# Cross attention and a mixture of LoRA experts: transfers in quarter tiles of 64 partitions with one of each kind in flight, and a fold of squares in wider matmuls

## The reference

```python
def xattn(q, k, v):                  # q = layernorm(x), k = v = ctx, 8 heads of 64 channels
    qh = softmax(q over the 64 channels of a head)
    kh = softmax(k over the 2048 positions)
    kvs = einsum('bnhd,bnhe->bhde', kh, vh)
    return einsum('bnhd,bhde->bnhe', qh, kvs)
x = x + xattn(layernorm(x), ctx, ctx)
flat = layernorm(x).reshape(-1, 2048)
logits = flat @ router_w.T           # 4 experts, the 2 largest kept, softmax over them: gates
mid = einsum('tf,erf->ter', flat, A) # rank 16 for each expert
x = x + einsum('te,teo->to', gates, einsum('ter,eor->teo', mid, B)) * 4
```

## Time and profile before

| what | value |
|---|---|
| median of 3 runs | 493.88 us (493.44 to 500.45) |
| the profiled execution, its own time | 496.45 us |
| its span | 494.7 us |
| mean granted TensorE clock | 0.92 of full speed |
| busy share PE, DVE, POOL, ACT | 84%, 77%, 73%, 61% |
| moved by DMA | 137.99 MB, mean 279 GB/s |

### The profile page before, as it was taken

The page is one execution under the profiler, slowest core; times in us unless marked ns, Lnnn a source line. Parts: engine busy times, 40 slices in busy tenths (PEclk is TensorE's granted clock), DMA queues, the critical chain, the costliest instruction groups (busy, mean ns, idle before and its releaser), DMA issues.

```text
span 494.7 us, 22911 instructions
## 1 busy us (share of the span) xinstructions
PE 416.6 (84%) x9960; PEld 362.5 (73%) x9960; DVE 378.6 (77%) x1045; ACT 300.2 (61%) x404; POOL 358.8 (73%) x341
## 2 busy tenths in 40 slices
PE   6659888988978887887988896898897878999975
PEld 6648777877867676776877675787776767788864
DVE  2488758896868967887897876868895978976864
ACT  1367767766648566574867665666674848586410
POOL 0459978987869767877797876867895987898510
PEclk9657978999989988999899997988998999999997
DMA  8997877899899888999899997899997998755347
GB/s 300 416 366 219 295 225 258 257 298 326 260 315 291 237 315 277 288 315 299 298 280 350 294 303 248 251 310 301 336 302 227 326 296 284 247 177 207 121 187 256
DMA packets 38996, 137.99 MB, mean 279 GB/s; under 512 B 4208, under 2 KB 6384, under 8 KB 38768
## 3 DMA queue, kind: packets, MB, share of 16 engines
q1 hardware_dynamic: 38896, 136.52, 82.3%
HBM read 102.95 MB, written 33.55 MB: 276 GB/s over the span
## 4 chain that ended last, share of the span: by engine, by line
PE 72%; issue 12%; DVE 7%; DMA 4%; SPq 3%; POOL 1%; ACT 1%; DVEq 0%; POOLq 0%
PE num_ps L404 17%; PE kv_ps L384 15%; PE raw_ps L421 13%; PE delta_ps L469 10%; PE kv_ps L436 7%; PE delta_ps L470 6%; DMA ctx_sb<-in_ctxt_dram 4%; DVE y_sb L705 2%; DVE attnT L696 2%; PE kv_ps L369 2%; SPq L234 1%; PE raw_ps L455 1%; PE num_ps L361 1%; DVE bn_parts L638 1%; SPq L229 1%
## 5 line engine op out<-in xcount | busy, mean ns | idle before, releaser
L322 POOL TENSOR_TENSOR y_sb<-attnT,y_sb 128x512 f32<-128x512 f32 x128 | 164.2, 1283 | 68.1 <-DVE attnT L696 67.4
L310 POOL TENSOR_TENSOR ek_sb<-ctx_sb,kmax_row 128x512 f32<-128x512 f32 x128 | 167.4, 1309 | 41.5 <-ACT kmax_row L502 40.8
L705 DVE TENSOR_TENSOR y_sb<-delta_ps,y_sb 128x512 f32<-128x512 f32 x128 | 87.4, 685 | 55.9 <-PE delta_ps L470 54.9
L404 PE MATMUL num_ps<-kv_sb,x_sb 64*64 64x65 f32 x4096 | 97.3, 233 | 18.4 <-issue 11.8
L384 PE MATMUL kv_ps<-ctx_sb,ek_sb 128*64 128x65 f32 x2048 | 100.3, 241 | 14.3 <-issue 14.0
L404 PEld LDWEIGHTS num_ps<-kv_sb,x_sb 64*64 64x64 f32 x4096 | 78.1, 142 | 34.2 <-issue 20.3
L384 PEld LDWEIGHTS kv_ps<-ctx_sb,ek_sb 128*64 128x64 f32 x2048 | 79.6, 146 | 28.4 <-issue 17.8
L421 PE MATMUL raw_ps<-w_sb,y_sb 128*64 128x69 f32 x2048 | 93.5, 232 | 6.8 <-issue 6.8
L621 DVE TENSOR_REDUCE max_n<-ctx_sb 128x32 f32<-128x512 f32 x128 | 86.4, 677 | 11.1 <-DMA ctx_sb<-in_ctxt_dram 11.1
L696 DVE TENSOR_TENSOR attnT<-num_ps,rden 128x512 f32<-128x512 f32 x128 | 88.5, 691 | 4.5
L469 PE MATMUL delta_ps<-midT,b_hi 128*128 128x256 f32 x256 | 84.2, 349 | 3.8 <-issue 3.1
(11 more groups left out here) (62 smaller groups left out, 423.6 us busy)
## 6 DMA issues: line engine op xcount, KB each, us to landing
ctx_sb<-in_ctxt_dram SPq DMA_DIRECT2D x64, 520.0 KB, 5.5
x_sb<-in_x_dram SPq DMA_DIRECT2D x64, 512.0 KB, 6.3
y_sb<-in_xt_dram SPq DMA_DIRECT2D x64, 512.0 KB, 6.5
out_dram<-y_sb SPq DMA_DIRECT2D x60, 512.0 KB, 6.0
out_dram<-y_sb SPq DMA_DIRECT2D x8, 256.0 KB, 3.6
sq_a<-in_bt_dram SPq DMA_DIRECT2D x1, 1024.0 KB, 15.8
w_sb<-in_wt_dram SPq DMA_DIRECT2D x1, 552.0 KB, 9.5
cst<-in_consts_dram SPq DMA_DIRECT2D x1, 145.0 KB, 2.4
```

Of the source, the lines that this page charges most:

```text
L310: pool.tensor_tensor(ek_sb[:, t % 2, chunks(g), :].rearrange("p (a b) c -> p a b c", b=2), ctx_sb[:, t % 4, 2 * g:2 * g + 2, 1:P + 1, :].r ...
L322: pool.tensor_tensor(y, attnT[:, g, :], y, ALU.add).then_inc(x1_made, 1)
L404: mm = pe.matmul(num_ps[n, h, j * (DH + 1):(j + 1) * (DH + 1)], x_sb[d, t % 4, c * P + half * DH:c * P + (half + 1) * DH], kv_sb[d, t % 2, ...
L705: dve.tensor_tensor(y, delta_ps[i % 2][:].rearrange("p (j t c) -> p t j c", j=2, t=2), y, ALU.add).then_inc(out_made, 1)
```

## The change

Two things change.

First, the transfers. A tile of each stream moves in four pieces: two halves of the row (`k`) by two halves of the partitions (`part`, 64 each). The pieces are 256 KB (260 KB for ctx). SP's loop has a step of one quarter, with one piece of each stream in it. Each piece waits until the previous piece of its own stream has landed (`out_piece`, `x_piece`, `xt_piece`, `ctx_piece`). The waits for PE change as well: store and y no longer wait for `raw_done`; x waits for `num_done` up to the quarter that PE runs at the same q; ctx is issued two quarters later in the loop (offset 14 for 16) and waits for `kv_done` of the quarter of the same q. The loads ahead of the loop are cut in the same four pieces, but without waits.

Second, the squares. `fold_squares` makes four matmuls of 384 columns (three chunks for each group of 32 partitions) and four of 128 columns that add the fourth chunk, into columns 128 to 511 of the bank. `sq_sum` has three parts of 128 columns, ACT copies 384 columns, and `sum_squares` has three matmuls for one.

The consumers' counts of landed pieces go from 32 to 64 for each use of a buffer; this is left out below.

```diff
         attnT = sb("attnT", [P, 4, W])
         sq_a = sb("sq_a", [P, 2, H2])
         sq_b = sb("sq_b", [P, H2])
-        sq_sum = sb("sq_sum", [P, 2, P])
+        sq_sum = sb("sq_sum", [P, 2, 3, P])
         junk = sb("junk", [P, N], BF16)
         max_n = sb("max_n", [P, 2, P])
         kmax = sb("kmax", [P, 2])
...
 
         @block.sync
         def _(sp):
-            PIECES = 2
-            CP = NCH // 2 // PIECES
-            XW = N // PIECES
-            YC = NCH // PIECES
-
-            def load_ctx(t, k):
+            XW = N // 2
+            CP = NCH // 4
+            YC = NCH // 2
+
+            def rows(part):
+                return slice(part * DH, (part + 1) * DH)
+
+            def load_ctx(t, k, part):
                 c = slice(k * CP, (k + 1) * CP)
-                sp.dma_start(ctx_sb[:, t % 4, c, :, :].rearrange("p a c b -> p a (c b)"),
-                             ctxt[t][:, c, :, :].rearrange("p a c b -> p a (c b)")).then_inc(ctx_landed[t % 4], 16)
-
-            def load_x(t, k):
+                sp.dma_start(ctx_sb[rows(part), t % 4, c, :, :].rearrange("p a c b -> p a (c b)"),
+                             ctxt[t][rows(part), c, :, :].rearrange("p a c b -> p a (c b)")
+                             ).then_inc(ctx_landed[t % 4], 16)
+
+            def load_x(t, k, part):
                 c = slice(k * XW, (k + 1) * XW)
-                sp.dma_start(x_sb[:, t % 4, c], x_rows[t * P:(t + 1) * P, c]).then_inc(x_landed[t % 4], 16)
-
-            def load_y(t, k):
+                sp.dma_start(x_sb[rows(part), t % 4, c], x_rows[t * P + part * DH:t * P + (part + 1) * DH, c]
+                             ).then_inc(x_landed[t % 4], 16)
+
+            def load_y(t, k, part):
                 c = slice(k * YC, (k + 1) * YC)
-                sp.dma_start(y_sb[:, t % 8, c, :], xt[t][:, c, :]).then_inc(y_landed[t % 8], 16)
-
-            def store(t, k):
+                sp.dma_start(y_sb[rows(part), t % 8, c, :], xt[t][rows(part), c, :]).then_inc(y_landed[t % 8], 16)
+
+            def store(t, k, part):
                 c = slice(k * YC, (k + 1) * YC)
-                sp.dma_start(out[t, :, c, :].rearrange("p j c -> p (j c)"),
-                             y_sb[:, t % 8, c, :].rearrange("p j c -> p (j c)")).then_inc(out_stored[t % 8], 16)
+                sp.dma_start(out[t, rows(part), c, :].rearrange("p j c -> p (j c)"),
+                             y_sb[rows(part), t % 8, c, :].rearrange("p j c -> p (j c)")
+                             ).then_inc(out_stored[t % 8], 16)
 
             def store_last(i):
                 c = slice(2 * i, 2 * i + 2)
...
                              ).then_inc(last_stored, 16)
 
             def whole(load, t):
-                for k in range(PIECES):
-                    load(t, k)
+                for k in range(2):
+                    for part in range(2):
+                        load(t, k, part)
 
             def quarters_done(q, offset):
...
             whole(load_y, 1)
             whole(load_x, 2)
             whole(load_ctx, 3)
-            STEP = 4 // PIECES
-            for q in range(0, 4 * NT + 28, STEP):
-                last = q + STEP - 1
-                p, r = divmod(q - 26, 8)
+            ctx_piece = x_piece = xt_piece = out_piece = (cst_landed, 16)
+            for q in range(0, 4 * NT + 28):
+                part = q % 2
+                p, r = divmod(q - part - 26, 8)
                 if 0 <= p < NP - 1:
-                    t, k = 2 * p + r // STEP % 2, r // (2 * STEP)
-                    after(sp, raw_done, quarters_done(q - 1, 7))
-                    sp.wait_ge(out_made, 8 * p + 8 // PIECES * (k + 1))
-                    store(t, k)
-                t, r = divmod(q + 10, 4)
+                    t, k = 2 * p + r // 2 % 2, r // 4
+                    sp.wait_ge(out_made, 8 * p + 4 * (k + 1))
+                    after(sp, *out_piece)
+                    store(t, k, part)
+                    out_piece = (out_stored[t % 8], 64 * (t // 8) + 32 * k + 16 * part + 16)
+                t, r = divmod(q - part + 10, 4)
                 if 3 <= t < NT:
-                    after(sp, num_done, 4 * (t - 4) + r + STEP)
-                    load_x(t, r // STEP)
-                t, r = divmod(q, 4)
+                    after(sp, num_done, 4 * (t - 4) + r + 2)
+                    after(sp, num_done, quarters_done(q, 5))
+                    after(sp, *x_piece)
+                    load_x(t, r // 2, part)
+                    x_piece = (x_landed[t % 4], 64 * (t // 4) + 16 * r + 16 * part + 16)
+                t, r = divmod(q - part, 4)
                 if 2 <= t < NT:
-                    after(sp, raw_done, quarters_done(q, 7))
                     if t >= 8:
-                        sp.wait_ge(out_stored[t % 8], 16 * PIECES * (t // 8))
-                    load_y(t, r // STEP)
-                t, r = divmod(q + 16, 4)
-                if t < NT:
-                    sp.wait_ge(kv_done, 4 * (t - 4) + r + STEP)
-                    load_ctx(t, r // STEP)
+                        sp.wait_ge(out_stored[t % 8], 64 * (t // 8))
+                    after(sp, *xt_piece)
+                    load_y(t, r // 2, part)
+                    xt_piece = (y_landed[t % 8], 64 * (t // 8) + 16 * r + 16 * part + 16)
+                t, r = divmod(q - part + 14, 4)
+                if 4 <= t < NT:
+                    sp.wait_ge(kv_done, 4 * (t - 4) + r + 2)
+                    after(sp, kv_done, quarters_done(q, 0))
+                    after(sp, *ctx_piece)
+                    load_ctx(t, r // 2, part)
+                    ctx_piece = (ctx_landed[t % 4], 64 * (t // 4) + 16 * r + 16 * part + 16)
             for i in range(8):
                 sp.wait_ge(out_made, 8 * (NP - 1) + i + 1)
                 store_last(i)
             for k in range(8):
                 uses = len(range(k, NT - 2, 8))
-                sp.wait_ge(out_stored[k], 16 * PIECES * uses)
+                sp.wait_ge(out_stored[k], 64 * uses)
             sp.wait_ge(last_stored, 16 * 8)
 
         @block.gpsimd
...
                 pe.wait_ge(sq_made, 2 * t + 2)
                 after(pe, kv_copied, min(t + 2, NT))
                 after(pe, row_made, min(t + 4, NT))
-                for k in range(NCH // 4):
-                    for s in range(4):
-                        sq = sq_b if k >= 2 else sq_a[:, t % 2, :]
-                        at = (4 * k + s) % 8 * P
-                        mm = pe.matmul(kv_ps[(t + 1) % 2][32 * s:32 * s + 32, 2 * P:3 * P], ones[:, 0:32],
-                                       sq[:, at:at + P], start=(k == 0), stop=(k == 3), skip_group_check=True)
+                to = kv_ps[(t + 1) % 2]
+                for s in range(4):
+                    sq = sq_b[:] if s >= 2 else sq_a[:, t % 2, :]
+                    at = s % 2 * 3 * P
+                    pe.matmul(to[32 * s:32 * s + 32, P:4 * P], ones[:, 0:32], sq[:, at:at + 3 * P],
+                              start=True, stop=False, skip_group_check=True)
+                for s in range(4):
+                    sq = sq_b[:] if s >= 2 else sq_a[:, t % 2, :]
+                    at = (6 + s % 2) * P
+                    mm = pe.matmul(to[32 * s:32 * s + 32, P:2 * P], ones[:, 0:32], sq[:, at:at + P],
+                                   start=False, stop=True, skip_group_check=True)
                 mm.then_inc(sq_folded, 1)
 
             def sum_squares(q):
...
                     return
                 p, odd = divmod(t, 2)
                 pe.wait_ge(sq_summed, t + 1)
-                pe.matmul(raw_ps[p % 2][:, odd, COL_SQ:COL_SQ + 2], sq_sum[:, t % 2, :], ones[:, 0:2],
-                          start=False, stop=True, skip_group_check=True).then_inc(sq_done, 1)
+                for k in range(3):
+                    mm = pe.matmul(raw_ps[p % 2][:, odd, COL_SQ:COL_SQ + 2], sq_sum[:, t % 2, k, :], ones[:, 0:2],
+                                   start=False, stop=(k == 2), skip_group_check=True)
+                mm.then_inc(sq_done, 1)
 
             def turn_mid(q):
                 p = pair_at(q, 15)
...
                     return
                 act.wait_ge(sq_folded, t + 1)
                 after(act, sq_done, t - 1)
-                act.activation(sq_sum[:, t % 2, :], kv_ps[(t + 1) % 2][:, 2 * P:3 * P], ACT.Copy,
+                act.activation(sq_sum[:, t % 2, :, :].rearrange("p k c -> p (k c)"), kv_ps[(t + 1) % 2][:, P:4 * P], ACT.Copy,
                                scale=1.0 / 32.0).then_inc(sq_summed, 1)
 
             def gate_exp(q):
```

More of the change, by code:

```diff
@@ L318, in add_x @@
                 if g == 0:
-                    pool.wait_ge(y_landed[t % 8], 32 * (t // 8 + 1))
+                    pool.wait_ge(y_landed[t % 8], 64 * (t // 8 + 1))
                 pool.wait_ge(attn_made, 4 * t + g + 1)
@@ L506, in sum_x @@
                     return
-                act.wait_ge(x_landed[t % 4], 32 * (t // 4 + 1))
+                act.wait_ge(x_landed[t % 4], 64 * (t // 4 + 1))
                 after(act, x_squared, t // 2)
```

(4 more changed lines are left out.)

## The result

The changed kernel takes 676.27 us (median of 5 runs, 670.59 to 688.99) against 493.94 us: ratio 1.366, 95% interval 1.360 to 1.372. It is slower, by 182 us, and outside the range of 440 to 550 us. The profiled execution took 688.99 us, 1.9% over that median.

What follows compares the result with a forecast made beforehand. PE with its issue stalls was taken as the bound. Quarters of 3.3 us for 3.57 us, times 102, gave 28 us off 496.5 us: 469 us, 466 us against the median, given as 467 us; range 440 to 550 us.

Steps and rivals of the forecast that it cites:

- What bounds the kernel now: First step: PE carries 72% of the chain; its issue stalls, 47 us from 60 to 410 us, read as late program blocks.
- under 5%: Sign of the forecast case: the chain's issue share falls from 14.5% to under 5% in the stretch with loads.
- landing time of 3.3 us: Transfers: time from a piece's issue to landing plus 0.1 us for SP, taken as the length of a quarter.
- The sum: Whole loop: quarters shorten from 3.57 to 3.3 us, times 102, 28 us off the profiled execution's 496.5 us.
- the spacing of SP's issues: SP's queue: issues 0.49 us apart leave 0.14 us of wait for each of three pieces ahead of a piece.
- upper end of 4.7 us: Landing wait: bound on a quarter if all three other pieces, 1.9 us, stand ahead of a 2.8 us load.
- Rival D: Landings: latency under load is larger at full rate, a small piece and a quarter take 4.1 us; 548 us, chance 0.10.
- 64 partitions run at the same rate: Loads ahead of the loop: condition for no cost there, with no waits and the same bytes.
- Rival B: Transfers: pieces on 64 partitions move at a lower rate, 208 GB/s if half; 518 to 580 us, middle 540, chance 0.25.
- The 1.12 us: Loads of y: time y was said to wait for `project` until now; after the change it follows x at once.
- the squares: Part 2, fold and `sum_squares`: net +0.2 us a tile, 6 us over 32 tiles if PE sets the pace.
- the clock: Sign of the forecast case: PE's mean clock rises over 0.94 in the loaded stretch.

Runs made afterwards that it cites:

- a_step2_two: Changed kernel with pieces of every second partition and two pieces of each stream in flight instead of one: 471.29 us, ratio 0.958 to the kernel before.
- b_squares: Kernel before with the change to the squares alone: 486.70 us, ratio 0.987.
- a_cols_two: Changed kernel with pieces of all 128 partitions by a quarter of a row, two of each stream in flight: 490.78 us, ratio 0.988.
- b_step2_squares: Kernel before with the new squares, each 512 KB piece issued as two on every second partition, old PE gates, no landing waits: 479.18 us, ratio 0.976.
- a_step2_nowait: Changed kernel with pieces of every second partition and without its four landing waits: 473.93 us, ratio 0.953 to the kernel before.
- a_nowait_alt: Changed kernel without landing waits, 64 neighbouring partitions, y taking the other half than x and ctx: 525.13 us.
- b_halves: Kernel before with each 512 KB piece issued as two of 64 neighbouring partitions, back to back, no landing waits: 544.91 us, ratio 1.103.
- a_two: Changed kernel on its 64 neighbouring partitions with two pieces of each stream in flight: 571.86 us, ratio 1.166 to the kernel before.
- a_nowait: Changed kernel on its 64 neighbouring partitions without its four landing waits: 572.77 us, ratio 1.167 to the kernel before.
- a_alt: Changed kernel, landing waits kept, with only the half that y takes changed: 657.13 us, ratio 1.331 to the kernel before.
- a_step2: Changed kernel with pieces of every second partition instead of 64 neighbours, all waits kept: 604.26 us, ratio 1.226 to the kernel before.
- a_step2_y: Changed kernel on every second partition with only the y stream's landing wait left: 551.27 us, ratio 1.113 to the kernel before.
- a_cols: Changed kernel with pieces of all 128 partitions by a quarter of a row, one in flight: 614.43 us, ratio 1.252.

## Why the prediction was wrong

*What bounds the kernel now* held, as far as the runs go: PE and its issue stalls. With two pieces of a stream in flight at the full rate (a_step2_two) PE's stalls fell by 31 us and the kernel by 23 us, to 471 us, near the forecast of 467 us. The stalls from 60 to 410 us stand by the landings of loads and stores as follows:

| kernel | landing, us | issue stalls of PE, us (times) |
|---|---|---|
| before | 5.3 to 6.6 | 47.3 (35) |
| b_squares | 5.6 to 6.6 | 39.8 (33) |
| a_cols_two | 5.2 to 5.9 | 38 (37) |
| b_step2_squares | 4.7 to 5.1 | 27.6 (23) |
| a_step2_nowait | 5.4 to 5.7 | 23.8 (21) |
| a_step2_two | 5.2 to 5.3 | 16.3 (22) |
| a_nowait_alt | 6.4 to 6.7 | 36.8 (28) |
| b_halves | 5.6 to 6.3 | 56.4 (38) |
| a_two | 7.3 to 7.8 | 53 (32) |
| a_nowait | 7.5 to 8.3 | 50.8 (31) |

They don't follow the landing time closely: b_halves lands its pieces in 5.6 to 6.3 us and stalls longest. The changed kernel shows none from 60 to 600 us, as forecast ("under 5%"), and the other runs that wait for the last piece of a stream (a_alt, a_step2, a_step2_y, a_cols) none or 0.7 us. PE isn't the bound in these, but nor is it in a_two and a_nowait, which stall over 50 us. So the stalls go away with these waits; that they are program blocks that come late was not tested. In the squares' run the instruction queue moved 76 packets for 79 and the stalls fell by 7.5 us; that this is where its gain comes from is argued and not shown.

*The step that failed first is the landing time of 3.3 us.* It is the term of the sum that was mis-sized, and it turned the sign. The sum took 3.3 us, of which 3.2 us were the landing and 0.1 us SP. At the full rate (a_step2) the landing measured 4.1 us, in a quarter of 4.28 us, and in the changed kernel itself 4.5 to 4.7 us in a quarter of 4.67 us. At 3.3 us a quarter would have been shorter than the 3.57 us of before; at 4.28 us it is longer. Of the 0.9 us, 0.3 us is the piece alone (3.1 us measured, 2.8 us by the line between two sizes) and 0.6 us is queueing, 1.0 us for the 0.4 us that I had from the spacing of SP's issues. That spacing was measured on one pair (ctx and store), and what the 1.0 us consists of stays open. The upper end of 4.7 us was worked out and then given to no rival, nor to the range; at 102 quarters it would have been some 610 us.

Rival D scaled the queueing that the trace showed and had 4.1 us. Its two parts, 2.8 and 1.3 us, measured 3.1 and 1.0 us, so that the sum was right is in part luck. Its 548 us fell short of 604 us for three reasons. The quarter is 4.28 us, 0.18 us more than the landing (18 us). The sum multiplied by the 102 quarters of one stretch, where the loop has 128 (19 us): from the first to the last projection matmul it took 430 us before and 522 us in a_step2 (43.8 to 565.7 us), 0.72 us a quarter more over all of them. And the end, from there to the last instruction, went from 22 to 38 us (16 us).

*The second is the choice that "64 partitions run at the same rate".* Rival B had it, at a chance of 0.25. The Trainium skill, "SBUF — State Buffer" (the DMA port swizzle), has it too, and the trace agrees (211 GB/s). B's rate of 208 GB/s was measured as 211, but its cost came in two parts, 51 us with the halves in turn and 99 us with three loads on one half. The order of the halves stood in the code and in B's own sentence ("all on the same half"), so the upper end was the better value.

*The rivals were taken as alternatives,* each with its own time, and the range ended inside one of them. D and B are separate causes and both happened: 604 and 573 us apart, 676 us together. No case had both. Each of them as measured already lies above 550 us, so the range was too narrow for either alone, too.

*Smaller readings.* The 1.12 us for which y is said to have waited runs from issue to issue; 0.33 us of it is the issue of x, so the wait was 0.79 us. SP's four issues take 0.47 us each and not 0.33 us. Neither changes the result.

*Right:* the moved gates at no cost that shows (474 us), ACT's wider copy (492 ns for 270 ns), the +0.42 us of `sum_squares` (0.45 us), its 192 records (L446 is L466 in the changed kernel), and the loads ahead of the loop as the place where B would show. *Wrong in sign:* the squares, which on the kernel before gained 7 us where 6 us more were forecast, and the clock, which fell to 0.83 from 60 to 600 us where it was to rise over 0.94. The reasons to expect the squares slower stand in the trace, so what gains more than they cost is open.

## What to carry to other kernels

A wait for the last transfer to land makes latency into pace. With one piece of each stream in flight a_step2 moved 1.05 MB in a quarter of 4.28 us, 245 GB/s, on a queue that had given 417 GB/s. Take the landing time under the load that the change leaves, not of a lone transfer, and keep two pieces of a stream in flight before anything else; with pieces of every second partition that made 471 us of 494 us. Where two rivals can both be true, price them together as well.

## What the runs showed of the hardware

- 64 neighbouring partitions load at 211 GB/s, the two halves in turn at 242 GB/s. Every second partition loads at up to 389 GB/s (417 GB/s over 12 us in a_step2) and is stored at 405 GB/s, all in runs of 4 KB. Two queues, one for each half, gave 251 GB/s, later 314 GB/s.
- Loads and stores together reach 322 to 324 GB/s on halves, on the same one or not, more than the 211 GB/s of loads alone on a half.
- The order of the halves in one queue was worth 48 us of 573 us.
- SP takes 0.47 us (median) to issue a piece of 64 partitions, neighbours or every second one, and 0.33 us for one of 128, of 256 KB or 512 KB.
- A 256 KB load takes 3.0 to 3.3 us alone, and 4.1 us with up to three others in flight (a_step2), although the mean from 60 to 410 us was only 238 GB/s and the same queue gave 417 GB/s from 13 to 25 us.
